# Nine layer norms worked in halves, squares on ScalarE, transposes copied straight to the held array

## The reference

```
def _layernorm(x, axis=-1, eps=1e-05):
    m = jnp.mean(x, axis=axis, keepdims=True)
    v = jnp.var(x, axis=axis, keepdims=True)
    return (x - m) / jnp.sqrt(v + eps)

h = embedding(tokens)                       # 16 x 128 x 192
h = h + retention(layernorm(h));  h = h + experts16(layernorm(h))
h = h + mamba(layernorm(h));      h = h + experts8(layernorm(h))
h = h + int8_attn(layernorm(h));  h = h + codebook_ffn(layernorm(h))
h = h + topk_attn(layernorm(h));  h = h + switch_ffn(layernorm(h))
```

```
mu = x.mean(-1, keepdims=True)
var = ((x - mu) ** 2).mean(-1, keepdims=True)
h = (x - mu) * jax.lax.rsqrt(var + EPS) * norm_w + norm_b
```

## Time and profile before

| | |
|---|---|
| median of the runs | 3940.85 us |
| profiled execution | 3947.3 us, its span 3945.4 us |
| PE busy | 2591.1 us, 66% |
| DVE busy | 2548.7 us, 65% |
| ACT busy | 1513.9 us, 38% |
| POOL busy | 895.5 us, 23% |
| mean granted TensorE clock | 0.806 of full speed |
| layer norm stages | 9, from 26.2 to 38.6 us, 277 us together |

### The profile page before, as it was taken

The page is one execution under the profiler, slowest core; times in us unless marked ns, Lnnn a source line. Parts: engine busy times, 40 slices in busy tenths (PEclk is TensorE's granted clock), DMA queues, the critical chain, the costliest instruction groups (busy, mean ns, idle before and its releaser), DMA issues. The chain is left out here.

```text
span 3945.4 us, 40861 instructions
## 1 busy us (share of the span) xinstructions
PE 2591.1 (66%) x13081; PEld 1614.0 (41%) x13128; DVE 2548.7 (65%) x5667; ACT 1513.9 (38%) x2746; POOL 895.5 (23%) x510
## 2 busy tenths in 40 slices
PE   2881999378888986599631112688989556665356
PEld 2771666233434333389411111323222445554345
DVE  4445232559999997211489997587787587787431
ACT  0000222166656652111114442677777244444211
POOL 2000000166776773367200000000000011011121
PEclk8775999689999997799855555899999777787568
DMA  1001100021111110511100000100000000000041
GB/s 34 8 7 39 67 0 0 28 86 43 43 43 43 43 43 0 148 40 39 46 0 0 0 0 1 50 1 1 1 1 1 28 1 1 1 1 1 25 133 48
DMA packets 59727, 108.45 MB, mean 27 GB/s; under 512 B 32253, under 2 KB 48091, under 8 KB 54331
## 3 DMA queue, kind: packets, MB, share of 16 engines
q1 hardware_dynamic: 53788, 94.44, 7.5%
q0 software_dynamic: 5760, 11.82, 1.0%
HBM read 92.17 MB, written 18.03 MB: 28 GB/s over the span
## 5 line engine op out<-in xcount | busy, mean ns | idle before, releaser
L1885 POOL TENSOR_TENSOR mam_st<-mam_du,mam_b_rows 128x1536 f32<-128x1536 f32 x128 | 439.4, 3439 | 172.1 <-PE mam_ysum L1954 171.6
L2115 DVE TENSOR_TENSOR_SCAN mam_st<-mam_da,mam_st 128x512 f32<-128x512 f32 x384 | 441.1, 1204 | 35.9 <-ACT mam_da L2055 18.2
L1650 DVE TENSOR_TENSOR cod_hp<-cod_hp,cod_gate 128x512 f32<-128x512 f32 x512 | 324.0, 681 | 122.5 <-ACT cod_hp L1517 120.5
L1954 PE MATMUL mam_ysum<-mam_st,held_ident 128*128 128x512 f32 x768 | 387.1, 644 | 2.2 <-DVE mam_st L2121 2.2
L1517 ACT ACTIVATE cod_hp<-cod_up,cod_b 128x512 f32<-128x512 f32 x512 | 318.8, 692 | 130.9 <-PE cod_up L1388 130.3
L2055 ACT ACTIVATE mam_da<-mam_delta,mam_decay 128x508 f32<-128x508 f32 x384 | 254.2, 683 | 184.7 <-DVE mam_st L2115 150.0
L2121 DVE TENSOR_TENSOR mam_st<-mam_st,mam_c_ps 128x1536 f32<-128x1536 f32 x128 | 224.4, 1753 | 17.2 <-PE mam_c_ps L1949 13.7
L470 DVE SCALAR_TENSOR_TENSOR held_h<-x_dn,held_gate,held_h 128x192 f32 x256 | 89.2, 410 | 225.2 <-PE x_dn L436 225.1
L1954 PEld LDWEIGHTS mam_ysum<-mam_st,held_ident 128*128 128x128 f32 x768 | 159.3, 207 | 169.3 <-issue 162.2
L425 PE MATMUL x_up<-x_xg,x_w 96*128 96x512 f32 x384 | 177.5, 600 | 55.4 <-ACTq L450 55.4
L311 POOL COPY held_xt<-n_cols 96x1024 f32 x32 | 34.3, 1074 | 776.3 <-ACT n_cols L292 776.3
(11 more groups left out here) (519 smaller groups left out, 5443.4 us busy)
## 6 DMA issues: line engine op xcount, KB each, us to landing
mam_b_rows<-b_scratch SPq DMA_DIRECT2D x32, 1024.0 KB, 7.5
sw_w<-in_L_w SPq DMA_DIRECT2D x2, 4608.0 KB, 33.2
gr_w<-in_L_w SPq DMA_DIRECT2D x1, 5376.0 KB, 43.0
x_w<-in_L_w SPq DMA_DIRECT2D x2, 2304.0 KB
gr_w<-in_L_w SPq DMA_DIRECT2D x1, 4608.0 KB
slot_scratch<-in_slot_fresh SPq DMA_DIRECT2D x1, 3860.0 KB
gr_rows<-slot_scratch SPq DMA_DIRECT2D x40, 96.5 KB, 1.9
gr_w<-home_scratch SPq DMA_DIRECT2D x16, 192.0 KB, 4.4
```

Source lines behind the costliest of these rows:

```text
L1650: nc.vector.tensor_tensor(at, at, gate[u % BANKS][:], ALU.mult).then_inc(gated, 1)
L1885: nc.gpsimd.tensor_tensor(st[it % N_ST][:], du[r % 2][:], along(b_rows[:, p % RING, n % PIECE, :], 1, [P, MC, MT]), ALU.mult)\
L1954: last = nc.tensor.matmul(ysum[:, c, :], m.ident[:], st[it % N_ST][:, c, :], start=False, stop=(it % DS == DS - 1))
L2115: nc.vector.tensor_tensor_scan(fs, fa, fs, 0.0, ALU.mult, ALU.add).then_inc(scanned, 1)
```

## The change

`norm_stage` is rewritten for all nine norms. VectorE works on two halves of 8 blocks: it centres both, then for each half sums the squares, makes the scales and scales two groups of rows. The squares are ScalarE activations. Rows are scaled in place in `xn`, so `rows`, `want_xn` and GpSimd's part fall away; TensorE turns from `xn`, with three PSUM buffers rather than two; ScalarE copies straight into `xt`. The loops are written out. TensorE's routes of a group stand behind the transposes of the next one. In the diff a run of more than three removed lines, which the listing above shows, is cut.

```diff
--- before.py
+++ after.py
@@ -174,8 +174,9 @@
     c.step(nc.vector.scalar_tensor_tensor(x, p, 1.0, bits.bitcast(F32), ALU.add, ALU.mult))
 
 
-def norm_stage(nc, m, a, name, src=None, router=None, n_routes=0, affine=None, want_xn=False, add_src=False):
+def norm_stage(nc, m, a, name, src=None, router=None, n_routes=0, affine=None, add_src=False):
     src = m.h if src is None else src
+    HB, RING = NB // 2, 3
     with Stage(nc, name) as s:
         sq = s.sb("sq", [P, NB, D])
         tot, runs = s.sb("tot", [P, NB]), s.sb("runs", [P, NB, D // 16])
@@ -183,25 +184,20 @@
         var = s.sb("var", [P, NB])
         std = s.sb("std", [P, NB])
         rstd = s.sb("rstd", [P, NB])
-        rows = [s.sb(f"rows{i}", [P, GS, D]) for i in range(2)]
-        cols = [s.sb(f"cols{i}", [DC, 2, GT]) for i in range(2)]
-        turned = [s.psum(f"turned{i}", [P, 2, 512]) for i in range(2)]
+        turned = [s.psum(f"turned{i}", [P, 2, 512]) for i in range(RING)]
         route_ps = [s.psum(f"route_ps{i}", [P, 512]) for i in range(2)]
         if router is not None:
             wr = s.sb("wr", [DC, 2, n_routes])
         if affine is not None:
             gain = s.sb("gain", [P, D])
             shift = s.sb("shift", [P, D])
...
+        names = "w_in dve centred squared var_ready std_ready rows_ready turned_ready cols_ready routed logits_kept"
+        (w_in, dve, centred, squared, var_ready, std_ready, rows_ready, turned_ready, cols_ready, routed,
+         logits_kept) = (s.sem(n) for n in names.split())
         block = s.block()
+
+        def half(k):
+            return slice(k * HB, (k + 1) * HB)
 
         @block.sync
         def _(sp):
@@ -215,101 +211,115 @@
         def _(v):
             c = Chain(v, dve)
 
...
+            def sums(x, at):
+                c.step(nc.vector.tensor_reduce(runs[:, at], x[:, at].rearrange("p t (r k) -> p t r k", k=16), AX.X,
+                                               ALU.add))
+                c.step(nc.vector.tensor_reduce(tot[:, at], runs[:, at], AX.X, ALU.add))
+
+            def centre(k):
+                at = half(k)
+                if add_src:
+                    c.step(nc.vector.tensor_tensor(m.h[:, at], m.h[:, at], src[:, at], ALU.add))
+                sums(src, at)
+                c.step(nc.vector.tensor_scalar(mean[:, at], tot[:, at], 1.0 / D, None, ALU.mult))
+                nc.vector.tensor_tensor(m.xn[:, at], src[:, at], along(mean[:, at], 2, [P, HB, D]), ALU.subtract)\
+                    .then_inc(centred, 1)
+
+            def spread(k):
+                at = half(k)
+                v.wait_ge(squared, k + 1)
+                sums(sq, at)
+                nc.vector.tensor_scalar(var[:, at], tot[:, at], 1.0 / D, LN_EPS, ALU.mult, ALU.add)\
+                    .then_inc(var_ready, 1)
+
+            def scales(k):
+                at = half(k)
+                v.wait_ge(std_ready, k + 1)
+                c.step(nc.vector.reciprocal(rstd[:, at], std[:, at]))
+                if affine is None:
+                    newton_steps(nc, c, rstd[:, at], var[:, at], std[:, at])
+
+            def rows(g):
+                at = slice(g * GS, (g + 1) * GS)
+                x = m.xn[:, at]
+                last = nc.vector.tensor_tensor(x, x, along(rstd[:, at], 2, [P, GS, D]), ALU.mult)
+                if affine is not None:
+                    c.step(last)
+                    c.step(nc.vector.tensor_tensor(x, x, along(gain[:], 1, [P, GS, D]), ALU.mult))
+                    last = nc.vector.tensor_tensor(x, x, along(shift[:], 1, [P, GS, D]), ALU.add)
+                last.then_inc(rows_ready, 1)
+
+            for k in range(2):
+                centre(k)
+            for k in range(2):
+                spread(k)
+                scales(k)
+                if affine is not None and k == 0:
+                    v.wait_ge(w_in, 32)
+                for g in range(k * NG // 2, (k + 1) * NG // 2):
+                    rows(g)
 
         @block.tensor
         def _(pe):
+            def turn(g):
+                pe.wait_ge(rows_ready, g + 1)
+                if g >= RING:
+                    pe.wait_ge(cols_ready, g - RING + 1)
+                for c in range(2):
+                    for t in range(GS):
+                        last = nc.tensor.transpose(turned[g % RING][0:DC, c, t * P:(t + 1) * P],
+                                                   m.xn[:, g * GS + t, c * DC:(c + 1) * DC], m.ident[:])
+                last.then_inc(turned_ready, 1)
+
+            def routes(g):
+                pe.wait_ge(cols_ready, g + 1)
+                if g >= 2:
+                    pe.wait_ge(logits_kept, g - 1)
+                for t in range(g * GS, (g + 1) * GS):
+                    for c in range(2):
+                        at = (t % GS) * n_routes
+                        last = nc.tensor.matmul(route_ps[g % 2][:, at:at + n_routes], m.xt[:, c, t * P:(t + 1) * P],
+                                                wr[:, c, :], start=(c == 0), stop=(c == 1))
+                last.then_inc(routed, 1)
+
             if router is not None:
                 pe.wait_ge(w_in, 16)
...
+            for g in range(NG):
+                turn(g)
+                if router is not None and g:
+                    routes(g - 1)
+            if router is not None:
+                routes(NG - 1)
 
         @block.scalar
         def _(act):
...
+            def keep_logits(g):
+                act.wait_ge(routed, g + 1)
+                nc.scalar.activation(m.logits[:, g * GS:(g + 1) * GS, 0:n_routes],
+                                     route_ps[g % 2][:, 0:GS * n_routes].rearrange("p (t e) -> p t e", e=n_routes),
+                                     ACT.Copy).then_inc(logits_kept, 1)
+
+            def root(k):
+                act.wait_ge(var_ready, k + 1)
+                nc.scalar.activation(std[:, half(k)], var[:, half(k)], ACT.Sqrt).then_inc(std_ready, 1)
+
+            def keep_cols(g):
+                act.wait_ge(turned_ready, g + 1)
+                nc.scalar.activation(m.xt[:, :, g * GT:(g + 1) * GT], turned[g % RING][0:DC], ACT.Copy)\
+                    .then_inc(cols_ready, 1)
+
+            for k in range(2):
+                act.wait_ge(centred, k + 1)
+                nc.scalar.activation(sq[:, half(k)], m.xn[:, half(k)], ACT.Square).then_inc(squared, 1)
+            root(0)
+            for g in range(NG):
+                if g == 1:
+                    root(1)
+                keep_cols(g)
+                if router is not None and g:
+                    keep_logits(g - 1)
+            if router is not None:
+                keep_logits(NG - 1)
 
 
 def rank_steps(nc, c, rank, work, tie, vals, E):
@@ -2156,7 +2166,7 @@
 
 
 def s_l1attn(nc, m, a):
-    norm_stage(nc, m, a, "n2", want_xn=True)
+    norm_stage(nc, m, a, "n2")
     norm_stage(nc, m, a, "n2b", src=m.xn, affine=("M_norm_w", "M_norm_b"), add_src=True)
     mamba_stage(nc, m, a)
 
@@ -2931,7 +2941,7 @@
 
 
 def s_l2attn(nc, m, a):
-    norm_stage(nc, m, a, "n4", want_xn=True)
+    norm_stage(nc, m, a, "n4")
     with Stage(nc, "quant") as s:
         z = Quant()
         z.x_int = s.sb("x_int", [P, NB, D], BF16)
@@ -3103,7 +3113,7 @@
 
 
 def s_l3ffn(nc, m, a):
-    norm_stage(nc, m, a, "n7", router="L3_router", n_routes=8, want_xn=True)
+    norm_stage(nc, m, a, "n7", router="L3_router", n_routes=8)
     gate_stage(nc, m, a, "g7", 8, 1, "tie8", True, bias="L3_rb", keep_probs=True)
     switch_stage(nc, m, a)
 
@@ -3124,7 +3134,7 @@
 
 
 def s_l1ffn(nc, m, a):
-    norm_stage(nc, m, a, "n3", router="L1_router", n_routes=8, want_xn=True)
+    norm_stage(nc, m, a, "n3", router="L1_router", n_routes=8)
     gate_stage(nc, m, a, "g3", 8, 2, "tie8", False, keep_rank=True)
     grouped_stage(nc, m, a)
```

More of the change, by code:

```diff
@@ L228, in _ @@
-            c.step(nc.vector.tensor_tensor(sq[:], m.xn[:], m.xn[:], ALU.mult))
-            sum_steps(sq)
-            nc.vector.tensor_scalar(var[:], tot[:], 1.0 / D, LN_EPS, ALU.mult, ALU.add).then_inc(var_ready, 1)
-            v.wait_ge(std_ready, 1)
-            c.step(nc.vector.reciprocal(rstd[:], std[:]))
[L233 to L237, removed]
@@ L259, in _ @@
             if router is not None:
                 pe.wait_ge(w_in, 16)
-            with pe.Fori(0, NG // 2) as i:
-                for k in range(2):
-                    pe.wait_ge(rows_ready[k], i + 1)
-                    pe.wait_ge(cols_ready[k], i)
-                    for c in range(2):
-                        for t in range(GS):
-                            last = nc.tensor.transpose(turned[k][0:DC, c, t * P:(t + 1) * P],
-                                                       rows[k][:, t, c * DC:(c + 1) * DC], m.ident[:])
-                    last.then_inc(turned_ready[k], 1)
-                if router is not None:
-                    for k in range(2):
-                        pe.wait_ge(cols_ready[k], i + 1)
-                        pe.wait_ge(logits_kept[k], i)
-                        for t in range(GS):
```

(18 more changed lines are left out.)

51 lines of the change are left out of this document (removed).

## The result

The changed kernel took 3909.55 us in the median (3904.26 to 3918.24, 4 runs) against 3941.19 us for the kernel before (3937.39 to 3946.7, 4 runs): a ratio of 0.9921, 95% interval 0.9896 to 0.9945. That is 31.6 us, where 30.9 were forecast. The profiled execution took 3918.24 us, the slowest of the four, span 3916.4 us against 3945.4 before.

A forecast was written before the change was run, and what follows sets the result against it. Nine norm stages, each a dependent chain closed by a barrier, were taken as what counts; gains of 19.2 (plain), 4.2 (n2b) and 7.5 (routers) sum to 30.9 us, from median 3940.85 to 3910, range 3893 to 3927.

The forecast's parts named there:

- The chain on VectorE: Dependent VectorE steps in each norm stage: last row group ends 19.69 us after the start, 20.2 with a load.
- the squares under cover: Squares moved to ScalarE run beside VectorE's work for free, taking 3.36 us off VectorE per stage.
- the table load: In n0, n2, n3, n6, n7 the load queues behind both squares, delaying the Sqrt 0.52 us, 2.6 in all.
- the end without GpSimd's copy: End of each plain stage: the last GpSimd copy, 1.04 us and its hand-over, goes.
- the plain stages: n0, n2, n4, n5, n6: to 23.3 us, 23.9 with a load; gains sum to 19.2 us.
- the router stages: n1, n3, n7: middle of fast and slow TensorE rates, 31.6 us, 32.1 with a load; gains sum to 7.5.
- the cost of splitting: VectorE in halves: nine or so extra fixed parts and second Newton steps, about 3.7 us, already in the sum.
- Rival C: Norm stages: squares slow VectorE, or the table switch costs its drain and more; gain 0 to 8 us; chance 0.05.
- the centring at 1.76 us beside the square: Sign in the norm stages that ScalarE's square does not slow VectorE: centring keeps its 1.76 us.
- rival A: Router stages: TensorE becomes the bound, all routes at 3.42 us; gain 18, 3922 us; chance 0.17.
- The working for the slow rate: Router stages: TensorE never idle from 12.98 us on, four turns of 1.98 and four routes end at 34.95 us.
- rival D: Expert and grouped stages: TensorE's level shifts, 0.8 us lost per us of full work at low level; slower; chance 0.03.

The follow-up runs named there:

- the second execution: The changed kernel run once more, unedited, against the kernel before: 3908.7 us, ratio 0.9912.
- the pairs: Changed kernel with TensorE's order as before, two turns then two route groups, against the changed kernel's single turns: 3910.2 us, ratio to the kernel before 0.9911.

## Why the prediction was right

The time (3909.6 for 3910) is nearer than its terms. The chain on VectorE, the squares under cover, the table load and the end without GpSimd's copy are as forecast. That the rest came to within 1 us is luck: the plain stages were 5.5 us better and the router stages 5.2 us worse than worked out.

- **The chain.** VectorE's last row group ended 19.63 us after the start in n0, forecast 20.2. The halved durations were exact (1.75, 0.25, 1.76); the 0.6 us are small savings that I had not counted, an independent instruction that starts before the one ahead has ended (43.67, the centring from 41.99 on taking 1.76) and 0.20 us for the reciprocal. The 3.7 us that the prediction names as the cost of splitting are too many: VectorE is busy 17.68 us in n0 with halves and 15.81 without, 1.9 us. The figure was no term of the sum.
- **The squares are free.** Right, and shown from both sides: back on VectorE they cost 30.3 us, on ScalarE without cover they gain 0.5 us a stage. Rival C's first half, contention with VectorE, did not occur: beside a square a large reduction takes 1.75 us and the addition of n2b 1.75. The sign that the prediction gave for it, the centring at 1.76 us beside the square, could not be seen, since the two do not overlap.
- **The table load.** The forecast idle time was 0.8 us, measured 0.92, so 0.64 us a stage for 0.52. The load follows the square after 0.02 us and the Sqrt follows it directly, as in the earlier trace rows. The drain of about 1380 ns that the Trainium skill, "ScalarE: Activation LUTs", section "What ACT_TABLE_LOAD costs", adds to each switch does not stand on the chain here. VectorE's whole idle time there is 0.92 us, and moving the load away gave back 0.64 of it.
- **GpSimd.** The tail was right, its slowing of VectorE larger than I had in mind for plain stages: 15.4 us for the copy to xt alone.
- **The turns.** Forecast 23.3 to 23.9 us for the plain stages, measured 21.9 to 23.3: 5.5 us better in the sum of five, half of it the earlier rows, the rest turns 2 and 3 of n2 and n6 at 1.95 us together.
- **The routers: this term was wrong.** I took the middle between the two rates, 31.6 to 32.1 us. All three ran at the low one, 33.3 to 33.9, and again in the second execution: rival A in its place, but not in its sum. The middle was a compromise between two rates and no mechanism, so it could not tell which stage would run how. The working for the slow rate, 34.95 us, was 1.7 above what n1 took, since it gives every turn 1.98 us, and a turn between routes adds 1.7 (329.69 less 326.28 us for two). The prediction also took the windows' granted clocks (0.61, 0.53, 0.63) as nearly the same; they are averages over stages in which TensorE mostly idles. Over the route groups of the earlier trace rows alone the clock before was 0.95, 0.50 and 0.93, as their durations say. A's reason, single turns between routes, is not what the pairs showed; and a stage whose TensorE code was that of before changed its level (n7, 32.4 to 37.9 us) as well. What ahead of a router stage sets its level stays open.
- **Outside the norm stages.** 2.7 us of the 31.7 came back in the profiled pair: spans of 29.0 apart. The stretches from n2b to n3 (mamba) and from n6 to n7 (top-k attention), before, then after:

```profile
765.21:1551.06 785.85, 649.40 (x1520) 281.23 (x1520) 674.48 (x553) 458.82 (x611) 513.47 (x161) 0.91 0.12 47
3094.67:3688.46 593.79, 358.81 (x2368) 298.20 (x2368) 424.81 (x2370) 250.83 (x786) 64.46 (x32) 0.77 0.02 5
```

```profile
750.52:1541.32 790.80, 657.35 (x1520) 283.17 (x1520) 674.76 (x554) 459.03 (x610) 513.59 (x161) 0.90 0.12 46
3059.63:3658.38 598.75, 361.53 (x2368) 300.85 (x2368) 424.80 (x2370) 250.97 (x786) 64.47 (x32) 0.77 0.02 5
```

VectorE's busy time is the same within 0.3 us, TensorE's is 8 and 3 us more, and the stages are 5 us longer each; the grouped experts and the codebook stage are 2.8 and 3.9 us shorter. In the other runs the mamba stage took 785 to 791 us and the attention 587 to 601, whatever the norm code was. So these differences are as large as the spread of those stages, and no price of the change can be seen in them. TensorE's share of it would be rival D in small, with both signs; what sets it is not shown.

## What to carry to other kernels

Work moved to an idle engine is worth what can run meanwhile, not what it weighed: make the second piece of work first (here by halves), then move. Do not add up what single parts of such a rewrite are worth: here the halves alone cost VectorE time, and the prices of taking out one part came to nearly twice the gain. When an activation of another kind is put ahead of one that needs a table, look where the load goes; one tiny early activation puts it back under cover. And a forecast of short bursts on TensorE needs both levels as bounds, since the same code came out at either.

## What the runs showed that I had not expected

TensorE's level can be bought with work that nothing reads: after 19 transposes a group of eight turns took 1.0 us rather than 1.9, and in a stage that TensorE waits in anyway this cost nothing. It did not last beyond the first routes and an idle time of 1.4 us (in n1 the next turn is back at 1.94 us). And GpSimd's copy lengthened not only large VectorE instructions but a 0.17 us step on 8 columns to 0.63 us.
